# Attention and MoE in one launch: the score fills and the small stages take turns on two PSUM banks, and the odd units of lone passes use the banks of the probability-value products

## The reference

```
def attn(x):                     # x: (8, 512, 256)
    xn = rms_norm(x, rms_w)
    q, k, v = (xn @ W).reshape(8, 512, 16, 16) for W in (Wq, Wk, Wv)
    scores = where(causal, q @ k.T / 16, -inf)
    return (softmax(scores) @ v).reshape(8, 512, 256) @ Wo + x

def ffn(x):                      # 2 experts, 1024 wide
    probs = softmax(x @ gate_w.T); sel = argmax(probs)
    g, u = x @ w_gate[sel].T, x @ w_up[sel].T
    return ((silu(g) * u) @ w_down[sel].T) * probs[sel]

x = x + 0.5 * ffn(layernorm(x))
x = x + attn(layernorm(x))
x = x + 0.5 * ffn(layernorm(x))
```

## Time and profile before

| | |
|---|---|
| Time, median of 3 runs | 1332.26 us (1330.32 to 1336.48) |
| Profiled execution: its time, its span | 1319.46 us, 1317.7 us |
| PE matmul busy | 1096.0 us, 83% of the span |
| DVE busy | 960.4 us, 73% |
| ACT busy | 711.8 us, 54% |
| POOL busy | 527.7 us, 40% |

### The profile page before, as it was taken

How to read it: one execution, slowest core, us unless ns; L and a number is a source line. 1 busy time by engine, 2 the same in 40 slices (tenths; PEclk the granted TensorE clock), 3 DMA queues, 4 the chain that set the end, 5 groups by cost and what they waited for, 6 DMA issues and landing times. The chain is left out here.

```text
span 1317.7 us, 39560 instructions
## 1 busy us (share of the span) xinstructions
PE 1096.0 (83%) x14564; PEld 946.3 (72%) x14564; DVE 960.4 (73%) x2040; ACT 711.8 (54%) x1331; POOL 527.7 (40%) x663
## 2 busy tenths in 40 slices
PE   0787789968999888888788898997979989788895
PEld 0766667757778776777676687876867878677784
DVE  6545547796888878878878887888878888675431
ACT  4434315655566565655655665675646655555321
POOL 3154443254523344443334533334543253343432
PEclk9898889998999899999899899998999999889998
DMA  9120352213221124123222141112422112311111
GB/s 319 58 81 26 105 93 60 86 54 86 74 83 48 34 70 114 39 66 91 69 75 74 54 126 51 39 57 67 100 74 61 52 51 72 82 47 42 50 45 45
DMA packets 115665, 96.16 MB, mean 73 GB/s; under 512 B 52288, under 2 KB 109376, under 8 KB 115488
## 3 DMA queue, kind: packets, MB, share of 16 engines
q1 hardware_dynamic: 98400, 66.88, 18.3%
q0 software_dynamic: 6144, 16.79, 4.3%
q10 hardware_dynamic: 10944, 9.97, 2.4%
HBM read 45.75 MB, written 37.88 MB: 63 GB/s over the span
## 5 line engine op out<-in xcount | busy, mean ns | idle before, releaser
L620 POOL TENSOR_TENSOR h_lo<-hid,h_hi 128x256 bf16<-128x256 f32 x304 | 221.2, 748 | 515.3 <-ACT h_hi L684 514.9
L760 ACT ACTIVATE area<-ps_st 128x512 f32<-128x512 f32 x320 | 190.5, 595 | 288.2 <-PE ps_st L1166 285.2
L953 DVE TENSOR_REDUCE row_min<-ps_s 128x1 f32<-128x512 f32 (+2 forms) x384 | 183.5, 505 | 79.2 <-PE ps_s L1145 78.0
L1077 PE MATMUL ps_g<-x_t,w 128*128 128x128 f16 x1104 | 211.5, 226 | 16.0 <-issue 8.8
L1079 PE MATMUL ps_u<-x_t,w 128*128 128x128 f16 x1104 | 211.5, 225 | 0.0
L1079 PE MATMUL ps_g<-x_t,w 128*128 128x128 f16 x1104 | 211.3, 226 | 0.0
L1077 PE MATMUL ps_u<-x_t,w 128*128 128x128 f16 x1104 | 211.1, 225 | 0.0
L1078 PE MATMUL ps_g<-x_t,w 128*128 128x128 f16 x1104 | 210.6, 225 | 0.0
L1078 PE MATMUL ps_u<-x_t,w 128*128 128x128 f16 x1104 | 209.9, 223 | 0.0
L971 DVE TENSOR_TENSOR area<-area 128x512 f16<-128x512 f32 x256 | 199.3, 779 | 9.7 <-ACT area L761 9.6
L1143 PE MATMUL ps_s<-kt,qt 96*128 96x512 bf16 (+3 forms) x512 | 139.6, 311 | 73.1 <-DVE row_min L953 56.8
(11 more groups left out here) (162 smaller groups left out, 2847.1 us busy)
## 6 DMA issues: line engine op xcount, KB each, us to landing
qk_scratch<-area SPq DMA_DIRECT2D x32, 384.0 KB, 2.6
qt<-qk_scratch SPq DMA_DIRECT2D x192, 64.0 KB, 2.7
kt<-qk_scratch SPq DMA_DIRECT2D x192, 64.0 KB, 2.7
y_sorted<-ys ACTq DMA_DIRECT2D x76, 128.0 KB, 1.7
x_buf<-x SPq DMA_DIRECT2D x8, 512.0 KB, 4.8
out<-x_buf SPq DMA_DIRECT2D x8, 512.0 KB, 2.9
x_sorted<-yt SPq DMA_DIRECT2D x18, 128.0 KB, 1.9
area<-w_down SPq DMA_DIRECT2D x4, 512.0 KB, 13.7
```

The lines of the kernel that those rows point to most:

```text
L620: pool.tensor_tensor(h_lo[:, u % 2, c], hid[:, u % 2, c], h_hi[:, u % 2, c], ALU.subtract).then_inc(h_lo_done, 1)
L760: act.activation(p_f32[:, f % 3], ps_st[:], ACT.Exp, scale=-1.0)
L953: ins = dve.tensor_reduce(row_min[:, p % 2, h + hh, i:i + 1], ps_s[:, at:at + P * (i + 1)], AX.X, ALU.min)
L1077: pe.matmul(cols, w_hi, x_hi, start=kb == 0 and f == 0, stop=False, skip_group_check=True)
```

## The change

All eight PSUM banks stay in use. `ps_s` and `ps_m` become `ps_w0` and `ps_w1`. S fills and small stages, 466 stages in PE's order (320 S fills and 146 small ones), take the two by turns: stage n writes `ps_w[n % 2]` and waits until stage n - 2 has been read. Counted in that order, 163 S fills stand behind two S fills and now wait for the reduction of the fill before last; 92 stand behind one small stage with an S fill ahead of it, and wait for the same reduction as before; 65 have a small stage two turns ahead, and wait until that one has been read. The odd units of lone passes use the banks `ps_v0` and `ps_v1` in place of `ps_s` and `ps_st`, and the one odd unit that was left out (unit 19, the last of pass 1) is now among them. The waits that tied S and `scores_t` to these units move to the first `pv`, and the wait of the late units is now for the last sum of PV's banks.

```
-SPARE = [u for u, (n, s, q) in enumerate(UNITS)
-         if q == 1 and n in (0, 1, len(PASSES) - 1) and (n, s) != (1, SLOTS[1] - 1)]
+SPARE = [u for u, (n, s, q) in enumerate(UNITS) if q == 1 and n in (0, 1, len(PASSES) - 1)]
...
-        ps_s, ps_st, ps_m = bank("ps_s"), bank("ps_st"), bank("ps_m")
+        ps_st = bank("ps_st")
+        ps_w = [bank(f"ps_w{n}") for n in range(2)]
...
-        free, last = {}, None
+        bank_of, free, turns = {}, {}, [None, None]
         for st in order:
-            if st[0] in ("transpose", "proj", "out_proj", "row_max", "l_prefix", "w_scale"):
-                free[st] = last
-                last = {...
+            if st[0] in ("transpose", "proj", "out_proj", "row_max", "l_prefix", "w_scale", "scores"):
+                n = len(free)
+                bank_of[st], free[st] = ps_w[n % 2], turns[n % 2]
+                turns[n % 2] = {...
+                                "scores": lambda p, f: (max_done, FILLS * p + f + 1)}[st[0]](*st[1:])
...
         def gate_bank(u):
-            return ps_s if u in SPARE else ps_g
+            return ps_v[0] if u in SPARE else ps_g
         def up_bank(u):
-            return ps_st if u in SPARE else ps_u
+            return ps_v[1] if u in SPARE else ps_u
...
                         elif u == FIRST_LATE:
-                            pe.wait_ge(*((max_done, FILLS * PARTS) if what == "gate" else (exp_done, FILLS * PARTS)))
+                            pe.wait_ge(o_summed, PAIRS * PARTS)
...
                 elif what == "scores":
-                    if FILLS * p + f:
-                        pe.wait_ge(max_done, FILLS * p + f)
-                    else:
-                        pe.wait_ge(gated, LAST_EARLY + 1)
...
                 elif what == "scores_t":
-                            pe.wait_ge(h_done, LAST_EARLY + 1)
...
                 elif what == "pv":
-                    if f % KINDS == 0 and n >= 2 * KINDS:
+                    if n == 0:
+                        pe.wait_ge(gated, LAST_EARLY + 1)
+                        pe.wait_ge(h_done, LAST_EARLY + 1)
+                    elif f % KINDS == 0 and n >= 2 * KINDS:
                         pe.wait_ge(o_summed, n // KINDS - 1)
```

More of the change, by code:

```diff
@@ L407, in macaron @@
         sets = {st[1:3]: n for n, st in enumerate([st for st in order if st[0] == "transpose" and st[3] == 0])}
-        free, last = {}, None
+        bank_of, free, turns = {}, {}, [None, None]
         for st in order:
-            if st[0] in ("transpose", "proj", "out_proj", "row_max", "l_prefix", "w_scale"):
-                free[st] = last
[L413 to L418, removed]
+            if st[0] in ("transpose", "proj", "out_proj", "row_max", "l_prefix", "w_scale", "scores"):
+                n = len(free)
+                bank_of[st], free[st] = ps_w[n % 2], turns[n % 2]
+                turns[n % 2] = {"transpose": lambda b, kind, kb: (xt_lo_done, 2 * sets[b, kind] + kb + 1),
+                                "proj": lambda b, m: (rest_done, NP * b + m + 1),
+                                "out_proj": lambda b, g: (x_c_ready, 2 * b + g + 1),
+                                "row_max": lambda p: (max_rows_done, p + 1),
+                                "l_prefix": lambda k, part: (l_pos, k + 1),
+                                "w_scale": lambda k: (w_scale_done, k + 1),
+                                "scores": lambda p, f: (max_done, FILLS * p + f + 1)}[st[0]](*st[1:])
         def lo_of(f):
@@ L630, in _ @@
             for st in order:
-                what = st[0]
+                what, ps = st[0], bank_of.get(st)
                 if what == "w_max" and st[1] >= GU_PIECES:
@@ L751, in _ @@
                         act.wait_ge(max_saved, 16 * p)
-                    act.activation(max_rows[:], ps_m[0:3 * HG * T, 0:P], ACT.Copy).then_inc(max_rows_done, 1)
+                    act.activation(max_rows[:], ps[0:3 * HG * T, 0:P], ACT.Copy).then_inc(max_rows_done, 1)
                 elif what == "exp":
@@ L1030, in _ @@
                     pe.wait_ge(w_max_done, k + 1)
-                    pe.transpose(ps_m[0:1, 0:P], w_max1[:, k:k + 1], ident[:]).then_inc(w_top_done, 1)
+                    pe.transpose(ps[0:1, 0:P], w_max1[:, k:k + 1], ident[:]).then_inc(w_top_done, 1)
                     pe.wait_ge(w_two_done, k + 1)
-                    pe.matmul(ps_m[:, 0:2], ones[0:1, :], w_two16[:], start=True, stop=True).then_inc(w_two_out, 1)
+                    pe.matmul(ps[:, 0:2], ones[0:1, :], w_two16[:], start=True, stop=True).then_inc(w_two_out, 1)
                 elif what == "l_prefix":
@@ L1045, in _ @@
                     for m in range(T):
-                        ins = pe.matmul(ps_m[:, m + 1:T + 1], ones[:], sel0[i][:, 0:T - m], start=False,
+                        ins = pe.matmul(ps[:, m + 1:T + 1], ones[:], sel0[i][:, 0:T - m], start=False,
                                         stop=m == T - 1, skip_group_check=True)
@@ L1110, in _ @@
                     for i in range(T):
[L1111 removed]
+                        ins = pe.transpose(ps[:, i * P:(i + 1) * P], src[:, i, kb * P:(kb + 1) * P], ident[:])
                     ins.then_inc(t_done, 1)
@@ L1128, in _ @@
                         at = (WQ if kind == "q" else WK) + g * P
-                        ins = three(ps_m[:], [(wa_hi[:, kb, at:at + P], wa_lo[:, kb, at:at + P]) for kb in range(KB)],
+                        ins = three(ps[:], [(wa_hi[:, kb, at:at + P], wa_lo[:, kb, at:at + P]) for kb in range(KB)],
                                     [(xt_hi[:, kb, :], xt_lo[:, kb, :]) for kb in range(KB)], True, True)
@@ L1142, in _ @@
                         keys = P * (i + 1)
-                        pe.matmul(ps_s[:, at:at + keys], qt[0:ROWS, h, i * P:keys], kt[0:ROWS, h, 0:keys],
+                        pe.matmul(ps[:, at:at + keys], qt[0:ROWS, h, i * P:keys], kt[0:ROWS, h, 0:keys],
                                   start=n == 0, stop=False, skip_group_check=True)
-                        ins = pe.matmul(ps_s[:, at + i * P:at + keys], ident16[:], mask_s[:], start=False, stop=True,
+                        ins = pe.matmul(ps[:, at + i * P:at + keys], ident16[:], mask_s[:], start=False, stop=True,
                                         skip_group_check=True)
@@ L1193, in _ @@
                         cols = slice(i * P, (i + 1) * P)
-                        ins = three(ps_m[:, t * D:(t + 1) * D],
+                        ins = three(ps[:, t * D:(t + 1) * D],
                                     [(xt_hi[:, kb, cols], xt_lo[:, kb, cols]) for kb in range(KB)],
```

35 lines of the change are left out of this document (18 added, 17 removed).

## The result

The changed kernel takes 1300.62 us (median of 4 runs, 1298.47 to 1305.59) against 1333.54 us for the kernel before (1330.32 to 1336.48) in the same comparison: a ratio of 0.9759, 95% interval 0.9721 to 0.9797, a gain of 33 us. Two more comparisons of the same pair, made beside the experiments, gave 0.9808 (0.9777 to 0.984) and 0.9776 (0.9745 to 0.9807). So the change is worth 1.9 to 2.4%. The predicted 1292 us were 40 us under the 1332.26 us of before.

A forecast was written before the change was run, and what follows sets the result against it. PE was taken to bound the S-fill stretch, DVE a close second, each waiting for the other at one bank. Terms 40 + 10 + 10 less 20 handed back gave 40 us off the 1332 us median: 1292 us, range 1262 to 1324.

The forecast's parts named there:

- The bound and the mechanism: In the S-fill stretch PE bounds, DVE a close second; S's wait for DVE's row minima, 72.9 us, is PE's largest idle time.
- the units' banks: At gate and up, unit 19 gets banks of its own; no wait for DVE there, so nothing, at most 1 us.
- The term of S: At S fills, a second bank removes 26 short stalls, 21.9 us, and shortens ten long ones, 18 us: together 40 us.
- The term of the small stages: At row_max, second transpose and early projections, small stages stop waiting for each other: half of 20.6 us, 10 us.
- The clock: On PE behind the ten long stalls, half become short enough to keep the clock: 10 us, ends 0 and 21.
- The handing back: Part of the waits returns at gate, pv or scores_t: a third of the gross, 20 us.
- 60 us gross: Over PE's S, small stages and clock, the gain before anything is handed back: 40 + 10 + 10 us.
- the full case: Rival: at S, nothing is handed back and the clock gives 21 us: 71 us gained, 1261 us; chance 0.14.
- S behind a small stage: 65 S fills wait from now on for a small stage; PE returns after two fills, 4 us: costed at nothing.
- The slower rival: S inherits small stages' readers, ACT and DVE, with 1 us of wait at 65 fills: 1357 us; chance 0.06.
- VectorE is the bound: Rival: DVE's backlog meets PE elsewhere, long stalls stay, two thirds of short ones go: 15 us, 1317 us; chance 0.22.

The follow-up runs named there:

- both waits put back: The change, with S waiting again for the reduction of the fill before and small stages for the last small one to be read: 1.0037 to the kernel before.
- small stages chained again: The change, with each small stage also waiting until the last small one has been read: 0.9914 to the kernel before.
- shorter blocks: DVE's four routing products stand 1 point apart on the list: 0.9921 on the kernel before, 0.9797 on the change, both to the kernel before.

## Why the prediction was right, point by point

**The bound and the mechanism: right.** S waiting for DVE was the largest idle time of PE, and freeing S and the small stages is the whole gain: with both waits put back the ratio is 1.0037, and the units' banks alone give 1.0009.

**The term of S, 40 us: right as a wait, too large as a gain.** PE's idle time before S fell from 73.1 to 24.0 us, by 49. But with S held back again and the rest of the change in place only 1.1% or 14 us were lost. The step that was mis-sized is "I take a third" for what is handed back: of 49 us less waiting some 14 us arrived, so it was some two thirds of this term. The rest shows in three places: at `l_prefix`, at `scores_t` (22.5 against 14.8 us), and in small waits at `gate` and `pv`.

**The term of the small stages, 10 us: too small.** It measured 1.1%, 14 us, give or take 5. Some 3.4 of these are early: S starts at 166.3 us where it started at 169.7, and at 168.9 with the small stages chained again. Its reasoning had a fault all the same. I wrote that small stages would wait "mostly for an S fill that has long been reduced". For `l_prefix` this is false: it stands behind DVE's own routing block, and the S fill two turns ahead is caught in that block. This new wait, 15.6 us of which 9.6 are owed to the turn, is the largest new wait in the trace, and I had not costed it. That taking it away would be a gain is not shown: with `l_prefix` later it was gone and the time was the same. A turn that a small stage takes is one that S's lead loses.

**The clock, 10 us: between 3 and 11.** No run isolates this term. The stretch's mean clock rose from 0.95 to 0.97, but in the two traces PE's busy time in it is the same (870.7 and 870.6 us), and over the whole execution it fell by 1096.0 - 1093.1 = 2.9 us. The traces of the two kernels taken once more differ by more, 1097.4 - 1086.0 = 11.4 us:

```profile
PE 1097.4 (83%) x14564; PEld 945.7 (72%) x14564; DVE 961.8 (73%) x2040; ACT 711.6 (54%) x1331; POOL 527.9 (40%) x663
...
PE 1086.0 (84%) x14564; PEld 937.9 (72%) x14564; DVE 963.6 (74%) x2040; ACT 712.6 (55%) x1331; POOL 529.6 (41%) x663
```

Part of the time at the lower clock lies in idle time and costs nothing, as in the first window of the earlier trace rows. The Trainium skill ("TensorE: Matmul & The Clock Gate", Part 1) gives its under 1% of the span for the ramp at a kernel's start. I took it for all that the clock could ever give, 13 us, which it does not say, and it does not describe the 0.95 of before, which comes from stalls all along the stretch.

**The handing back, 20 us: too small**, as said, for the terms taken at their full waits. Of the 60 us gross some half came back, not a third. By the experiments the two freedoms are worth 30 us together, less some 5 us that the turns cost, and the change measured 26 us in that set (1322.3 - 1295.9) and 33 us in the first comparison. The forecast of 40 us was high by 7 to 14.

**Where it was luck.** I read all terms from an execution of 1319.5 us and carried the 40 us over to a median of 1332. In the set where the kernel before took 1322 us, the level of the trace that I read, the gain was 26 us and would have missed the 28 to 53 us of my forecast; at 1333 us it was 31 and 33. The term of S less all that I let be handed back was 20 us and measured 14, that of the small stages was 10 and measured 14: the two misses offset each other in part. In the range, I counted most of the full case in, but that case's own 1261 us lies outside 1262, so about half of its chance at most could count, not 0.11 of 0.14.

**What was costed at nothing was nothing:** the units' banks (1.0009), and S behind a small stage. In the trace of the change S waits for `xt_lo`, `area` L924 and `area` L929 for 0.9 + 1.3 + 0.5 us:

```profile
PE ps_w L1143 <- DVE area L924: 1.3, 1, 1.3
...
PE ps_w L1143 <- DVE xt_lo L916: 0.9, 4, 0.2
...
PE ps_w L1143 <- DVE area L929: 0.5, 1, 0.5
```

The slower rival is out with that. The rival "VectorE is the bound" had a true part: backlog met PE elsewhere, and moving `l_prefix` alone only moved the wait. It is not the total of DVE's work that does it: the kernel with shorter blocks and a later `l_prefix` has nearly the same work on DVE (801.9 us in its stretch, 810.2 in that of before, 1731 instructions in both) and is 0.7% faster than the change beside it (1294.3 against 1302.9 us).

## What to carry to other kernels

A wait view adds up what an engine lost at a place, not what a cure at that place returns. Where two engines run in one fixed order, ask which stage behind the freed one depends on the same late engine; here that was the next user of the shared banks itself. A second buffer lets the engine in front run one stage further ahead, 2.07 us here, and a block of some 6 us on the other engine outlasts that. The buffer alone gave 1.9 to 2.4%, the shorter blocks with `l_prefix` later 1.2%, and all of it together 2.9%; on top of the buffer neither of the two moves gave anything alone. When buffers are taken by turns among stages of several kinds, every kind uses up the lead of the others: here 163 of 320 S fills got a longer one.

## What the runs showed of the hardware

A stall that is shorter did not always save the clock. In the long stall of before the window had 0.73 already and the one behind it 0.51; in the change, whose first wait there is 3.07 us, the clock still stood at 1.00 in the stall's window and fell to the lower level only behind it, where the window's mean is 0.61. These are the two windows of the changed kernel:

```profile
441.00:445.60 4.60, 0.65 (x12) 0.39 (x9) 4.53 (x13) 0.94 (x3) 1.79 (x2) 1.00 0.39 117
445.60:450.00 4.40, 4.36 (x42) 3.31 (x43) 2.98 (x9) 1.08 (x2) 0.00 (x0) 0.61 0.00 0
```

The same routing product on DVE takes 0.42 us or over 2 us in one block: 2.24 us in the earlier trace rows, 2.28 us in the trace of the change, right behind one of 0.42. Of the 64 products in that trace 47 took 0.43 us or less and 17 took 0.77 to 2.28 us. POOL was at work for most of each long one, here with this instruction:

```profile
437.93 2.13 POOL L570 TENSOR_TENSOR xs<-xn_f,xs 128x1024 f16<-128x1024 f32 x1 [1.50 <-ACT xs L668]
```

POOL was also at work beside some of the short ones, and that it is the cause was not tried.

The kernel before took 1321 to 1322 us in two sets of runs and 1333 to 1335 us in three others, and one chip gave both, 1322.3 and 1335.3 us. In the trace of the change (1301.5 us) PE idles for "issue" before plain gate and up matmuls, 5.0 us at L1083 alone, waits that the trace of its faster execution (span 1295.4 us) does not have at that line. Whether this makes the two levels is open; there is no trace of the kernel before at its longer time.
